# Expert weights fetched by GpSimd's indirect DMAs in place of the sync engine's queue, with GpSimd's loop written out

## The chip, the core and the metric

The kernel runs on one core of a Trainium2 chip. The metric is device time in microseconds (us), from the first to the last instruction of one execution. Five engines take part, each with its own instruction stream: TensorE (PE, the matmuls), VectorE (DVE), ScalarE (ACT), GpSimd (POOL) and the sync engine (SP, which here only issues DMAs). They wait for each other through semaphores.

## What is computed

Six blocks work on 2048 token vectors of 128 numbers: a mixture of experts, causal attention, the mixture again, a block with windowed attention and 32 experts, an encoder block, and the window block once more. The change touches the 32 experts of the window block, which therefore run twice. Cut to what matters, with `h2` the normed tokens:

```python
glogits = h2 @ gate_w + gate_b
topv, topi = jax.lax.top_k(glogits, TOPK)              # 4 of 32 experts for each token
gw = jax.nn.softmax(topv, axis=-1)
combine = zeros((N, 32)).at[arange(N)[:, None], topi].add(gw)
def body(acc, we):                                     # one expert: W_up[e], W_down[e], combine[:, e]
    wu, wd, ce = we
    ug = h2 @ wu                                       # 128 -> 256
    u, g = ug[:, :128], ug[:, 128:]
    return acc + ce[:, None] * (silu(g) * u @ wd), None
y2, _ = jax.lax.scan(body, zeros_like(h2), (W_up, W_down, combine.T))
```

Every expert is applied to every token, and `combine` (mostly zeros) weighs the result.

## The kernel before

Tokens lie along the free axis, in four chunks of 512 (`NCH`, `NC`). A **step** of `experts` (line 541) is one expert on one chunk, so an expert has four steps, and 32 experts have 128. Steps are numbered here from the start of an even expert: steps 0 to 3 are its own, 4 to 7 those of the next expert. Each step keeps fp32 precision by splitting every operand into a high and a low part and adding three products.

- **PE**, line 660, `up`: six matmuls into `gate_up` (two buffers); line 675, `down`: three matmuls that add to `y`. In the loop `up(j+3)` stands ahead of `down(j)`. `up` waits for the product of two steps before (line 656) and, at an expert's first step, for `w_low` (line 654); `down` waits for the low part of `hidden` (lines 669 to 673).
- **ACT**, in each step: `silu(j+1)` (line 696), then the high part of `hidden` of step j, `high(j)` (line 714). At an expert's first step it also makes `w_high` of the next expert (line 703), after a wait for that expert's weights; at its third step `down_high` (line 708).
- **DVE**, in each step: the product of the two halves (line 737); in odd steps the low part of the step before, `low(j-1)` (line 598); then the multiplication by the expert's share, `hidden(j)` (line 744).
- **POOL**: in odd steps `low(j)` (line 598), after a wait for `high(j)`; at an expert's first step `w_low` of the next expert (line 375), at its third `down_low` (line 380). It runs a loop over pairs of experts, with the last pair written out.
- **SP**: for each expert the two parts of its weights (`ExpertParts.load`, lines 346 and 349, 128 KB and 64 KB) and the 1 MB broadcast of its share (line 617). Each is sent when its slot of two is free: the weights when the low parts of the expert two before have been made, the share when `hidden` of that expert is done.

The router (line 388), which runs just ahead, loads and cuts expert 0 through `load_first`, `high_of_first` and `low_of_first`. `mixture` uses the same functions for 8 larger experts and a shared one; there the change leaves all as it is.

Of the kernel before, what the change touches and what calls it, by code (L numbers as in the profile page):

```python
# [14 lines left out]
U32 = mybir.dt.uint32  # L15
# [18 lines left out]
class Phase:  # L34
# [4 lines left out]
    def __init__(self, nc, tag):  # L39
        self.nc, self.tag = nc, tag  # L40
# [283 lines left out]
class ExpertParts:  # L324

    def __init__(self, phase, weights, halves):
        self.weights, self.pieces = weights, halves
        self.width, self.down_width = halves * 256, halves * 128  # L330
# [8 lines left out]
        self.down_loaded = [phase.sem(f"down_loaded{s}") for s in range(2)]  # L339
        self.w_high_done, self.w_low_done = phase.sem("w_high_done"), phase.sem("w_low_done")  # L340
        self.down_high_done, self.down_low_done = phase.sem("down_high_done"), phase.sem("down_low_done")

    def load(self, sp, k, slot):
# [5 lines left out]
        sp.dma_start(self.w_down[slot][:], self.weights[bass.ds(k, 1), :, self.width:].rearrange(  # L349
            "e p c -> (e p) c")).then_inc(self.down_loaded[slot], 16)  # L350

    def load_first(self, sp):
        sp.dma_start(self.w[0][:], self.weights[0, :, 0:self.width]).then_inc(self.w_loaded[0], 16)
        sp.dma_start(self.w_down[0][:], self.weights[0, :, self.width:]).then_inc(self.down_loaded[0], 16)

# [185 lines left out]
def experts(nc, tag, sbuf, parts, x, combine_dram, halves, routed, shared, inner=None):  # L541
# [9 lines left out]
    steps = NCH * halves  # L551
# [3 lines left out]
    CUT_AT, CUT_DOWN_AT = 0, 2 * halves  # L555
    with Phase(nc, tag) as p:
# [31 lines left out]

        def last(it, j):

            return isinstance(it, int) and j == left - 1

        def cut_hidden(engine, it, j):

# [17 lines left out]
        @block.sync  # L612
        def _(sp):
            def load_share(k, slot):

                sp.wait_ge(hidden_done, (k - 1) * steps + EXPERT_CREDIT)
                sp.dma_start(share[slot][:], combine_dram[bass.ds(k, 1), :].to_broadcast(
                    [128, T])).then_inc(share_loaded[slot], 16)

            sp.dma_start(share[0][:], combine_dram[0:1, :].to_broadcast([128, T])  # L620
                         ).then_inc(share_loaded[0], 16)
            with sp.Fori(0, pairs - 1) as it:
                for after in (1, 2):
                    parts.load(sp, it * 2 + after, after % 2)
                    load_share(it * 2 + after, after % 2)
            for k in range(routed - 1, total):
                parts.load(sp, k, k % 2)
                load_share(k, k % 2)

        @block.gpsimd  # L630
        def _(pool):
# [61 lines left out]
        def _(act):  # L693
            def silu(it, j):
                act.wait_ge(gate_up_done, it * (2 * steps) + j + 1)
                act.activation(gated[j % SLOTS][:], gate_up[j % 2][:, 0, :], ACT.Silu  # L696
                               ).then_inc(silu_done, 1)

            def cut_weights(loaded, k, slot):

                act.wait_ge(w_loaded[slot], loaded * 16)

                act.activation(w_high[slot][:], w[slot][:], ACT.Copy).then_inc(w_high_done, 1)

            def cut_down(loaded, k, slot):
                act.wait_ge(down_loaded[slot], loaded * 16)
# [433 lines left out]
            dve.wait_ge(added, NCH)  # L1140


def window_block(nc, tag, sbuf, dram, x, h):

    with Phase(nc, tag) as p:
        u = p.sb("u", [128, T])
# [868 lines left out]
def build(nc, dram, out):  # L2015
    Phase.cleared = []
    with ExitStack() as stack:
        sbuf = {}
        for name, shape, dt in [
            ("x", [128, T], F32), ("ident", [128, 128], F32), ("mean_w", [128, 128], F32),  # L2020
            ("zero_bf", [128, NC], BF16), ("iota", [128, 32], F32),
            ("moe_gate", [128, 8], F32), ("moe_bias", [128, 8], F32),
            ("win_norm", [128, 2], F32), ("win_gate", [128, 32], F32), ("win_gate_b", [128, 32], F32),
        ]:
            sbuf[name] = stack.enter_context(nc.sbuf_tensor(name, shape, dt))
        x = sbuf["x"]
# [5 lines left out]
        window_block(nc, "g1", sbuf, dram, x, h)  # L2032
        encoder_block(nc, "b1", sbuf, dram, x, h)
        window_block(nc, "g2", sbuf, dram, x, h)
        with Phase(nc, "store") as p:
            stored = p.sem("stored")
            block = p.block()
# [7 lines left out]
def host_arrays(i):  # L2045

    a = {}
# [97 lines left out]
```

## Time and profile before

| | |
|---|---|
| time, median of 2 runs | 2673.74 us (2672.32 to 2675.15) |
| the profiled execution, span from its first to its last instruction | 2676.0 us |
| PE busy | 2414.5 us (90%) |
| DVE busy | 2018.5 us (75%) |
| ACT busy | 1425.3 us (53%) |
| POOL busy | 831.3 us (31%) |
| the two runs of the 32 experts | about 1150 to 1420 us and 2400 to 2670 us of the span |
| steady state in them, PE's three `down` matmuls of one step to those of the next | 2.04 us, so 8.16 us an expert |

In the page an idle time is followed by what ended it. Busy shares are means over the whole span; what an edit in the experts is worth is read from a stretch inside them. The profile gives no time of its own beside the span; the span is 2.3 us above the median of the runs.

### The profile page before, as it was taken

How to read it: one execution, taken by the hardware profiler on the slowest of the kernel's cores; microseconds unless marked ns; L12 is line 12 of the kernel's file. 1: busy time of each engine (PE TensorE's matmuls, PEld its weight loads, DVE VectorE, ACT ScalarE, POOL GpSimd, SP SyncE). 2: the span in 40 equal slices, each digit the busy share in tenths (PEclk: the TensorE clock that was granted, in tenths of full speed). 3: DMA queues.
4: the chain of work that ended last, by engine and by line, in shares of the span. 5: the costliest groups of instructions: out<-in, count | busy, mean ns of one | idle time of the engine just before them, and what ended most of it. 6: DMA issues, size and time to landing. Idle time of an engine off the chain costs nothing. (4 is left out here: it accounts for less than half of the span.)

```text
span 2676.0 us, 39008 instructions
## 1 busy us (share of the span) xinstructions
PE 2414.5 (90%) x12429; PEld 1458.6 (55%) x12429; DVE 2018.5 (75%) x4042; ACT 1425.3 (53%) x3042; POOL 831.3 (31%) x813
## 2 busy tenths in 40 slices
PE   9995999869988999899996599999669899989998
PEld 6872333248865555478884422222146555458887
DVE  5985777449988999278886188888349899639888
ACT  4652456626623877156664047667511578526665
POOL 3644222216544000146665100000006200016665
PEclk9997899989999999899998789999889999989999
DMA  2213111022130000034442601010222000014443
GB/s 90 86 38 100 30 42 42 7 86 87 59 87 5 1 1 1 11 135 157 156 148 53 168 17 40 22 40 5 35 44 64 5 1 1 9 44 150 149 149 125
DMA packets 104852, 166.68 MB, mean 62 GB/s; under 512 B 55170, under 2 KB 77570, under 8 KB 92850
## 3 DMA queue, kind: packets, MB, share of 16 engines
q1 hardware_dynamic: 87812, 162.77, 19.4%
q10 hardware_dynamic: 16896, 2.10, 0.5%
q8 instruction: 77, 1.26, 0.2%
q14 instruction: 67, 0.55, 0.1%
HBM read 145.36 MB, written 12.78 MB: 59 GB/s over the span
## 5 line engine op out<-in xcount | busy, mean ns | idle before, releaser
L1623 DVE TENSOR_REDUCE b1x_maxima<-b1x_m_bank 128x1 f32<-128x512 f32 x512 | 319.3, 683 | 59.6 <-PE b1x_m_bank L1557 58.7
L1643 ACT ACTIVATE b1x_probs<-b1x_e_bank 128x1024 f32<-128x1024 f32 x256 | 248.3, 1021 | 143.9 <-PE b1x_e_bank L1574 143.8
L1623 DVE TENSOR_REDUCE a1x_maxima<-a1x_m_bank 128x1 f32<-128x512 f32 (+3 forms) x384 | 191.3, 549 | 59.6 <-PE a1x_m_bank L1560 30.7
L1643 ACT ACTIVATE a1x_probs<-a1x_e_bank 128x1024 f32<-128x1024 f32 (+1 forms) x192 | 146.2, 812 | 132.1 <-PE a1x_e_bank L1574 131.9
L1557 PE MATMUL b1x_m_bank<-b1a_k_slot,b1a_q_slot 96*128 96x512 bf16 x512 | 186.7, 404 | 12.1 <-DMA b1a_q_slot<-scratch_q_parts 11.9
L1574 PE MATMUL b1x_e_bank<-b1a_q_slot,b1a_k_slot 128*128 128x512 bf16 x512 | 153.8, 383 | 1.5 <-DMA b1a_q_slot<-b1x_max_parts 0.5
L1557 PE MATMUL a1x_m_bank<-a1a_k_slot,a1a_q_slot 96*128 96x512 bf16 (+3 forms) x384 | 120.6, 351 | 21.3 <-POOL a1x_mask L1508 12.1
L1589 PE MATMUL b1x_o_bank<-b1x_probs,b1a_v_aug 128*32 128x512 f32 x1024 | 136.4, 605 | 0.4 <-ACT b1x_probs L1643 0.4
L598 POOL TENSOR_TENSOR g1e_low<-g1e_hidden,g1e_high 128x512 fp32r<-128x512 f32 x63 | 109.3, 1735 | 82.0 <-ACT g1e_high L714 82.0
L598 POOL TENSOR_TENSOR g2e_low<-g2e_hidden,g2e_high 128x512 fp32r<-128x512 f32 x63 | 109.3, 1735 | 82.0 <-ACT g2e_high L714 82.0
L1557 PEld LDWEIGHTS b1x_m_bank<-b1a_k_slot,b1a_q_slot 96*128 96x128 bf16 x512 | 41.6, 97 | 167.8 <-DVE b1x_maxima L1623 128.9
L744 DVE TENSOR_TENSOR g1e_hidden<-g1e_hidden,g1e_share 128x512 f32<-128x512 f32 x128 | 114.0, 890 | 3.5 <-DMA g1e_share<-scratch_combine 1.2
L744 DVE TENSOR_TENSOR g2e_hidden<-g2e_hidden,g2e_share 128x512 f32<-128x512 f32 x128 | 114.0, 890 | 3.5 <-DMA g2e_share<-scratch_combine 1.1
L696 ACT ACTIVATE g2e_gated<-g2e_gate_up 128x512 f32<-128x512 f32 x128 | 76.6, 598 | 70.7 <-PE g2e_gate_up L660 70.7
L696 ACT ACTIVATE g1e_gated<-g1e_gate_up 128x512 f32<-128x512 f32 x128 | 76.6, 598 | 70.7 <-PE g1e_gate_up L660 70.7
L1515 POOL CAST b1x_max_parts<-b1x_rest 16x128 bf16<-16x128 f32 x16 | 4.5, 281 | 352.4 <-DVE b1x_rest L1619 352.4
L737 DVE TENSOR_TENSOR g2e_hidden<-g2e_gate_up,g2e_gated 128x512 f32<-128x512 f32 x128 | 87.6, 685 | 25.5 <-ACT g2e_gated L696 25.3
L737 DVE TENSOR_TENSOR g1e_hidden<-g1e_gate_up,g1e_gated 128x512 f32<-128x512 f32 x128 | 87.6, 685 | 25.4 <-ACT g1e_gated L696 25.3
L660 PE MATMUL g1e_gate_up<-g_h_high,g_w_high 128*128 128x512 f32 x256 | 100.2, 391 | 1.0 <-DVE g1e_hidden L737 1.0
L660 PE MATMUL g2e_gate_up<-g_h_high,g_w_high 128*128 128x512 f32 x256 | 100.1, 391 | 1.0 <-DVE g2e_hidden L737 1.0
L1528 POOL TENSOR_SCALAR_AFFINE_SELECT a1x_probs<-a1x_probs 128x256 f32<-128x256 f32 x128 | 51.4, 407 | 156.9 <-ACT a1x_probs L1643 156.2
L660 PE MATMUL g2e_gate_up<-g_h_low,g_w_high 128*128 128x512 f32 x256 | 99.6, 389 | 0.0
(598 smaller groups left out, 6750.7 us busy)
## 6 DMA issues: line engine op xcount, KB each, us to landing
g1e_share<-scratch_combine SPq DMA_DIRECT2D x32, 1024.0 KB, 4.9
g2e_share<-scratch_combine SPq DMA_DIRECT2D x32, 1024.0 KB, 4.9
f1e_share<-scratch_combine SPq DMA_DIRECT2D x9, 1024.0 KB, 4.8
f2e_share<-scratch_combine SPq DMA_DIRECT2D x9, 1024.0 KB, 4.8
g_w<-in_win_experts SPq DMA_DIRECT2D x64, 128.0 KB, 4.4
b1e_window<-scratch_bias_table SPq DMA_DIRECT2D x16, 320.0 KB, 4.6
f_w<-in_moe_w SPq DMA_DIRECT2D x18, 256.0 KB, 4.8
a1a_k_slot<-scratch_k_parts SPq DMA_DIRECT2D x24, 192.0 KB
```

The costliest lines, as they stand in the source:

```text
L598: engine.tensor_tensor(low[s][:], hidden[s][:], high[s][:], ALU.subtract).then_inc(low_done[j % BY_POOL == BY_POOL - 1 and not last(it, j) ...
L660: mm = pe.matmul(gate_up[j % 2][:, which, :], a[slot][:, at], b[:, chunk(n)], start=(part == 0), stop=(part == 2))
L696: act.activation(gated[j % SLOTS][:], gate_up[j % 2][:, 0, :], ACT.Silu).then_inc(silu_done, 1)
L737: dve.tensor_tensor(hidden[s][:], gate_up[j % 2][:, 1, :], gated[s][:], ALU.mult).then_inc(product_done, 1)
L744: dve.tensor_tensor(hidden[s][:], hidden[s][:], share[slot][:, chunk(n)], ALU.mult).then_inc(hidden_done, 1)
L1515: pool.tensor_copy(into[:, 0, :], rest[:]).then_inc(cut, 1)
L1528: pool.affine_select(square, square, [[0, 2], [1, 128]], ALU.is_ge, 0.0, base=0, channel_multiplier=-1).then_inc(cleared, 1)
L1557: mm = pe.matmul(bank[:, 0:width], q_slot[s][0:MAX_ROW, qt // 4, hh, chunk(qt % 4, 128)], k_slot[s][0:MAX_ROW, hh, k0:k0 + width], start=T ...
L1574: mm = pe.matmul(e_bank[pair][:, a, 0:width], k_slot[s][:, hh, chunk(kt, 128)], q_slot[s][:, qh, hh, lo - qh * NC:], start=True, stop=True)
L1589: mm = pe.matmul(o_bank[32 * hh:32 * hh + 32, at:at + width], v_aug[:, half // 2, kt, chunk(hh, 32)], probs[u % 2][:, hh, 0:width], start= ...
L1623: dve.tensor_reduce(maxima[:, k0 // NC, col:col + 1], bank[:, 0:width], AX, ALU.max).then_inc(m_taken, 1)
L1643: act.activation(probs[u % 2][:, 2 * pair:2 * pair + 2, 0:width], e_bank[pair][:, :, 0:width], ACT.Exp, scale=scale).then_inc(exp_done, 1)
```

## The change

`ExpertParts` gets two tables in device memory for the window block's experts: `win_up`, 32 x 128 rows of 256 numbers, and `win_down`, 32 x 128 rows of 128. A new SBUF tensor, `expert_rows`, loaded at the program's start, holds for expert k in column k the 128 row numbers. `gather`, run by GpSimd, fetches the weights of expert k by two indirect DMAs, each of which takes a row number for each of the 128 partitions. Expert 0 is still loaded by SP. SP keeps the shares. GpSimd's program for these experts is written out over all 128 steps in place of the loop; the gathers of expert k+2 stand in expert k's third step, behind `down_low`. Two pairs of semaphores that are never cleared count the gathers, so the second window block adds the counts of the first.

```diff
+    def gather(self, pool, rows, k, slot):
+        pool.wait_ge(self.w_low_done, self.pieces * (k + 1))
+        pool.indirect_dma_start(out=self.w[slot][:], out_offset=None, in_=self.tables[0][:, :],
+                                in_offset=bass.IndirectOffsetOnAxis(ap=rows[:, k:k + 1], axis=0)
+                                ).then_inc(self.w_gathered[slot], 16)
+        pool.wait_ge(self.down_low_done, k + 1)
+        pool.indirect_dma_start(out=self.w_down[slot][:], out_offset=None, in_=self.tables[1][:, :],
+                                in_offset=bass.IndirectOffsetOnAxis(ap=rows[:, k:k + 1], axis=0)
+                                ).then_inc(self.down_gathered[slot], 16)
...
             with sp.Fori(0, pairs - 1) as it:
                 for after in (1, 2):
-                    parts.load(sp, it * 2 + after, after % 2)
+                    if parts.tables is None:
+                        parts.load(sp, it * 2 + after, after % 2)
                     load_share(it * 2 + after, after % 2)
...
-            pair_steps(pool, step)
+            if parts.tables is None:
+                pair_steps(pool, step)
+                return
+            parts.gather(pool, sbuf["expert_rows"], 1, 1)
+            for k in range(total):
+                for j in range(k % 2 * steps, k % 2 * steps + steps):
+                    step(k // 2, j, k + 1 if k + 1 < total else None)
+                    if j % steps == CUT_DOWN_AT and k + 2 < total:
+                        parts.gather(pool, sbuf["expert_rows"], k + 2, k % 2)
...
             def cut_weights(loaded, k, slot):
-                act.wait_ge(w_loaded[slot], loaded * 16)
+                if parts.tables is None:
+                    act.wait_ge(w_loaded[slot], loaded * 16)
+                else:
+                    act.wait_ge(parts.w_gathered[slot], loaded_after_first(loaded, slot) * 16 + parts.gathered_before[slot])
                 act.activation(w_high[slot][:], w[slot][:], ACT.Copy).then_inc(w_high_done, 1)
...
-        parts = ExpertParts(p, dram["win_experts"], halves=1)
+        parts = ExpertParts(p, None, halves=1, tables=(dram["win_up"], dram["win_down"]),
+                            gathered=gathered)
...
-    a["win_experts"] = f(np.concatenate([up[:, :, 128:], up[:, :, :128], g("W_down")], axis=2))
+    a["win_up"] = f(np.concatenate([up[:, :, 128:], up[:, :, :128]], axis=2).reshape(32 * 128, 256))
+    a["win_down"] = f(g("W_down").reshape(32 * 128, 128))
+    a["expert_rows"] = (np.arange(128)[:, None] + 128 * np.arange(32)[None, :]).astype(np.uint32)
```

On POOL, inside the first window block's experts, the loop body of one pair of experts stood so before (`g_w_low` and `g_down_low` are the next expert's low parts, `g1e_low` is `low(j)` of an odd step):

```order
L375 TENSOR_TENSOR g_w_low<-g_w,g_w_high 128x256
L597 ISA
L598 TENSOR_TENSOR g1e_low<-g1e_hidden,g1e_high 128x512
L380 TENSOR_TENSOR g_down_low<-g_w_down,g_down_high 128x128
L597 REGISTER_ALU
L598 TENSOR_TENSOR g1e_low<-g1e_hidden,g1e_high 128x512
L374 REGISTER_ALU
```

These rows are the first of the two experts. With the change the block begins with the gathers of expert 1, and then the first expert's steps stand so:

```order
L358 DMA g_w<-in_win_up,expert_rows 128x256
L362 DMA g_w_down<-in_win_down,expert_rows 128x128
L393 TENSOR_TENSOR g_w_low<-g_w,g_w_high 128x256
L616 TENSOR_TENSOR g1e_low<-g1e_hidden,g1e_high 128x512
L398 TENSOR_TENSOR g_down_low<-g_w_down,g_down_high 128x128
L358 DMA g_w<-in_win_up,expert_rows 128x256
L362 DMA g_w_down<-in_win_down,expert_rows 128x128
L616 TENSOR_TENSOR g1e_low<-g1e_hidden,g1e_high 128x512
```

Two DMAs have come between `down_low` and the `low` of each expert's last step; the register instructions and the branch of the loop are gone.

On SP, in the same block, half of the loop body was this before:

```order
L346 ISA
L346 DMA g_w<-in_win_experts 128x256
L349 ISA
L349 DMA g_w_down<-in_win_experts 128x128
L616 ISA
L617 ISA
L617 DMA g1e_share<-scratch_combine 128x2048
```

With the change the whole body for two experts is this:

```order
L640 ISA
L635 ISA
L635 DMA g1e_share<-scratch_combine 128x2048
L634 ISA
L635 ISA
L635 DMA g1e_share<-scratch_combine 128x2048
L640 REGISTER_ALU
L640 COMPARE_AND_BRANCH
```

Only the shares are left on SP's queue.

## Rows read from the trace of the kernel before

**Rows 1.** The page's first lines: span, then busy time, share and instructions by engine.

```profile
span 2676.0 us, 39008 instructions
...
PE 2414.5 (90%) x12429; PEld 1458.6 (55%) x12429; DVE 2018.5 (75%) x4042; ACT 1425.3 (53%) x3042; POOL 831.3 (31%) x813
```

**Rows 2.** Stretches inside the experts: length, busy time by engine, PE's granted clock, DMA.

```profile
core 0: us, PE busy (x) PEld busy (x) DVE busy (x) ACT busy (x) POOL busy (x), PEclk, DMA share, GB/s
1225.00:1290.00 65.00, 65.00 (x289) 53.81 (x288) 57.97 (x80) 41.39 (x81) 42.61 (x33) 1.00 0.44 153
...
2410.00:2660.00 250.00, 249.78 (x1102) 206.43 (x1101) 223.04 (x307) 159.63 (x307) 165.05 (x123) 1.00 0.42 149
```

**Rows 3.** Who waited for whom, 1160 to 1410 us: total, times, longest.

```profile
POOL g1e_low L598 <- ACT g1e_high L714: 80.1, 62, 1.3
...
PE g1e_y L675 <- POOL g1e_low L598: 0.2, 1, 0.2
```

**Rows 4.** Timeline of PE, two matmuls: start, length, line, tiles.

```profile
1230.54 0.39 PE L675 MATMUL g1e_y<-g1e_high,g_down_high 128*128 128x512 f32 x1
...
1238.70 0.39 PE L675 MATMUL g1e_y<-g1e_high,g_down_high 128*128 128x512 f32 x1
```

**Rows 5.** Timeline of POOL over one expert: start, length, idle before and releaser.

```profile
1226.05 0.90 POOL L380 TENSOR_TENSOR g_down_low<-g_w_down,g_down_high 128x128 fp32r<-128x128 f32 x1
1228.24 1.74 POOL L598 TENSOR_TENSOR g1e_low<-g1e_hidden,g1e_high 128x512 fp32r<-128x512 f32 x1 [1.29 <-ACT g1e_high L714]
1230.20 1.02 POOL L375 TENSOR_TENSOR g_w_low<-g_w,g_w_high 128x256 fp32r<-128x256 f32 x1 [0.21 <-ACT g_w_high L703]
1232.51 1.74 POOL L598 TENSOR_TENSOR g1e_low<-g1e_hidden,g1e_high 128x512 fp32r<-128x512 f32 x1 [1.29 <-ACT g1e_high L714]
1234.21 0.90 POOL L380 TENSOR_TENSOR g_down_low<-g_w_down,g_down_high 128x128 fp32r<-128x128 f32 x1
```

**Rows 6.** Timeline of DVE over the same expert.

```profile
1226.56 0.94 DVE L744 TENSOR_TENSOR g1e_hidden<-g1e_hidden,g1e_share 128x512 f32<-128x512 f32 x1
1227.42 0.68 DVE L737 TENSOR_TENSOR g1e_hidden<-g1e_gate_up,g1e_gated 128x512 f32<-128x512 f32 x1
1228.14 0.69 DVE L744 TENSOR_TENSOR g1e_hidden<-g1e_hidden,g1e_share 128x512 f32<-128x512 f32 x1
...
1229.94 0.68 DVE L598 TENSOR_TENSOR g1e_low<-g1e_hidden,g1e_high 128x512 fp32r<-128x512 f32 x1
1230.54 1.23 DVE L744 TENSOR_TENSOR g1e_hidden<-g1e_hidden,g1e_share 128x512 f32<-128x512 f32 x1
1231.69 0.68 DVE L737 TENSOR_TENSOR g1e_hidden<-g1e_gate_up,g1e_gated 128x512 f32<-128x512 f32 x1
1232.40 0.69 DVE L744 TENSOR_TENSOR g1e_hidden<-g1e_hidden,g1e_share 128x512 f32<-128x512 f32 x1
```

**Rows 7.** POOL's subtractions: count, shortest, median and longest in ns.

```profile
L598 POOL TENSOR_TENSOR g1e_low<-g1e_hidden,g1e_high x63: 1289/1740/1821, 1159.2 to 1411.5; 128x512 fp32r<-128x512 f32 x63
...
L380 POOL TENSOR_TENSOR g_down_low<-g_w_down,g_down_high x64: 457/903/930, 1134.2 to 2656.1; 128x128 fp32r<-128x128 f32 x64
```

**Rows 8.** SP's issues of the weights (ns), and these weights' landing.

```profile
L346 SPq DMA_DIRECT2D g_w<-in_win_experts x62: 332/333/738, 1150.8 to 2642.0; - x62
...
DMA to landing us min/median/max: 2.1/4.4/6.9
```

**Rows 9.** Timeline of SP's queue over the same expert.

```profile
1227.67 0.33 SPq L617 DMA_DIRECT2D g1e_share<-scratch_combine  x1
1228.54 0.33 SPq L346 DMA_DIRECT2D g_w<-in_win_experts  x1
```

**Rows 10.** Timeline of ACT over the same expert.

```profile
1229.71 0.41 ACT L703 ACTIVATE g_w_high<-g_w 128x256 fp32r<-128x256 f32 x1
1230.74 0.60 ACT L696 ACTIVATE g1e_gated<-g1e_gate_up 128x512 f32<-128x512 f32 x1 [0.61 <-PE g1e_gate_up L660]
1231.80 0.63 ACT L714 ACTIVATE g1e_high<-g1e_hidden 128x512 fp32r<-128x512 f32 x1 [0.46 <-DVE g1e_hidden L744]
```

**Rows 11.** Timeline of the first window block's start, ACT and POOL.

```profile
1156.49 0.40 ACT L703 ACTIVATE g_w_high<-g_w 128x256 fp32r<-128x256 f32 x1
...
1156.97 0.94 POOL L375 TENSOR_TENSOR g_w_low<-g_w,g_w_high 128x256 fp32r<-128x256 f32 x1 [22.29 <-ACT g_w_high L703]
```

**Rows 12.** Timeline of the program's start: the last two loads of constants.

```profile
3.67 0.43 SPq L108 DMA_DIRECT2D win_gate<-in_win_gate  x1
...
4.15 0.43 SPq L108 DMA_DIRECT2D win_gate_b<-in_win_gate_b  x1
```

More of the change, by code:

```diff
@@ L324, with __init__ @@
 class ExpertParts:
-    def __init__(self, phase, weights, halves):
+    def __init__(self, phase, weights, halves, tables=None, gathered=None):
         self.weights, self.pieces = weights, halves
+        self.tables = tables
         self.width, self.down_width = halves * 256, halves * 128
@@ L339, in __init__ @@
         self.down_loaded = [phase.sem(f"down_loaded{s}") for s in range(2)]
+        if tables is not None:
+            self.w_gathered, self.down_gathered, self.gathered_before = gathered
         self.w_high_done, self.w_low_done = phase.sem("w_high_done"), phase.sem("w_low_done")
@@ L350, in load @@
             "e p c -> (e p) c")).then_inc(self.down_loaded[slot], 16)
+    def gather(self, pool, rows, k, slot):
[7 more added lines that the diff above has]
+                                ).then_inc(self.down_gathered[slot], 16)
     def load_first(self, sp):
+        if self.tables is not None:
+            sp.dma_start(self.w[0][:], self.tables[0][0:128, :]).then_inc(self.w_loaded[0], 16)
+            sp.dma_start(self.w_down[0][:], self.tables[1][0:128, :]).then_inc(self.down_loaded[0], 16)
+            return
         sp.dma_start(self.w[0][:], self.weights[0, :, 0:self.width]).then_inc(self.w_loaded[0], 16)
@@ L589, in last @@
         def last(it, j):
-            return isinstance(it, int) and j == left - 1
+            return isinstance(it, int) and it == (total - 1) // 2 and j == left - 1
         def cut_hidden(engine, it, j):
@@ L623, in _ @@
                 for after in (1, 2):
-                    parts.load(sp, it * 2 + after, after % 2)
+                    if parts.tables is None:
+                        parts.load(sp, it * 2 + after, after % 2)
                     load_share(it * 2 + after, after % 2)
             for k in range(routed - 1, total):
-                parts.load(sp, k, k % 2)
+                if parts.tables is None:
+                    parts.load(sp, k, k % 2)
                 load_share(k, k % 2)
@@ L639, in step @@
                     cut_hidden(pool, it, j)
-            pair_steps(pool, step)
+            if parts.tables is None:
+                pair_steps(pool, step)
+                return
+            parts.gather(pool, sbuf["expert_rows"], 1, 1)
[4 more added lines that the diff above has]
+                        parts.gather(pool, sbuf["expert_rows"], k + 2, k % 2)
         @block.tensor
@@ L697, in silu, with loaded_after_first @@
                                ).then_inc(silu_done, 1)
+            def loaded_after_first(loaded, slot):
+                return loaded - 1 if slot == 0 else loaded
             def cut_weights(loaded, k, slot):
-                act.wait_ge(w_loaded[slot], loaded * 16)
+                if parts.tables is None:
+                    act.wait_ge(w_loaded[slot], loaded * 16)
+                else:
+                    act.wait_ge(parts.w_gathered[slot], loaded_after_first(loaded, slot) * 16 + parts.gathered_before[slot])
                 act.activation(w_high[slot][:], w[slot][:], ACT.Copy).then_inc(w_high_done, 1)
             def cut_down(loaded, k, slot):
-                act.wait_ge(down_loaded[slot], loaded * 16)
+                if parts.tables is None:
+                    act.wait_ge(down_loaded[slot], loaded * 16)
+                else:
+                    act.wait_ge(parts.down_gathered[slot], loaded_after_first(loaded, slot) * 16 + parts.gathered_before[slot])
                 act.wait_ge(down_done, k * steps - steps + EXPERT_CREDIT)
@@ L1140, in _, with window_block @@
             dve.wait_ge(added, NCH)
-def window_block(nc, tag, sbuf, dram, x, h):
+def window_block(nc, tag, sbuf, dram, x, h, gathered):
     with Phase(nc, tag) as p:
@@ L2023, in build @@
             ("win_norm", [128, 2], F32), ("win_gate", [128, 32], F32), ("win_gate_b", [128, 32], F32),
+            ("expert_rows", [128, 32], U32),
         ]:
@@ L2031, in build @@
         mixture(nc, "f2", sbuf, dram, x, h)
-        window_block(nc, "g1", sbuf, dram, x, h)
+        w_gathered = [nc.alloc_semaphore(f"w_gathered{s}") for s in range(2)]
+        down_gathered = [nc.alloc_semaphore(f"down_gathered{s}") for s in range(2)]
+        window_block(nc, "g1", sbuf, dram, x, h, (w_gathered, down_gathered, (0, 0)))
         encoder_block(nc, "b1", sbuf, dram, x, h)
-        window_block(nc, "g2", sbuf, dram, x, h)
+        window_block(nc, "g2", sbuf, dram, x, h, (w_gathered, down_gathered, (15 * 16, 16 * 16)))
         with Phase(nc, "store") as p:
```

## The prediction

> **What bounds the kernel now.** I read the busy shares first: PE 90% of the span, POOL 31% [rows 1]. A mean over six blocks does not say what the 32 experts wait for, so the next view is that of stretches inside them. There PE is busy for 65.00 of 65.00 us, and for 249.78 of 250 us in the second window block, at a granted clock of 1.00, which is the 2.4 GHz level; POOL works 42.61 of 65 us [rows 2]. The table of waits says the same from the other side: in 250 us PE waited once, for 0.2 us, on POOL's `low`, while POOL waited 62 times for ACT's `high`, 80.1 us in all, 1.3 us each [rows 3]. So the experts are bound by PE, and the loads that the change takes from SP cost PE nothing today. A gain can hardly come out of them. What the change can do is use up POOL's waiting, and the question is how much of it there is at the place where the gathers stand.
>
> The timelines of one expert answer that. PE starts `down(3)` at 1230.54 and `down(7)` at 1238.70, so an expert takes 8.16 us [rows 4]. POOL ends `down_low` at 1226.05 + 0.90 = 1226.95, waits 1.29 us for ACT's `high(3)`, and starts `low(3)` at 1228.24 [rows 5]. That `low(3)` takes 1.74 us, though the shortest of its kind takes 1.289 us [rows 7]. The DVE row beside it says why: `hidden(4)` starts at 1228.14 and ends at 1228.83 [rows 6], and 1228.83 + 1.15 = 1229.98 is where `low(3)` ends. The same shows the other way: DVE's `hidden(5)` takes 1.23 us where `hidden(4)` takes 0.69, and it ends 0.55 us behind the end of POOL's `w_low` at 1231.22 [rows 5, 6]. POOL's subtractions and those DVE operations whose inputs both lie in SBUF hold each other up for whole instructions; the DVE product of line 737, which reads PSUM, is not held up. The Trainium skill has this as a rule ("SBUF — State Buffer", the section on engine contention: a DVE instruction with two SBUF inputs contends with a GpSimd instruction that reads SBUF, and the later one waits); the trace agrees.
>
> **The chain through POOL.** From one `down_low` to the next the work is tied together: `low(3)`, then DVE's `low(4)`, which waits for it, `w_low`, `hidden(5)`, which waits for that, product(6), `hidden(6)` (1232.40, 0.69), `low(5)`, which gets on only at 1233.09 and ends at 1234.25, DVE's `low(6)`, and the next `down_low`, which ends at 1235.11 [rows 5, 6]. From 1226.95 that is 8.16 us. The only slack on POOL's side of this ring is between 1226.95 and 1228.83, when `low(3)` really gets going: 1.88 us. Two gathers that together take G us are hidden up to G = 1.88; each microsecond beyond moves `low(3)`, and with it the rest of the ring, by one. PE's own margin does not help twice: `low(3)` ends at 1229.98 and `down(3)` starts at 1230.54 [rows 4, 5], 0.56 us that are used up once, at the first expert or two, while the ring loses time at each expert.
>
> **The change, part by part.**
>
> *The gathers' time on POOL.* No row of this trace has a DMA issued by POOL, so g, the time of one gather, is bounded. From below: SP issues the same load in 0.333 us [rows 8]. From above: the longest instruction that POOL repeats here, 1.74 us [rows 5]. For what lies between I go by POOL's own rows: undisturbed, 128 columns take 0.457 us and 512 take 1.289 us [rows 7]. I count a gathered row as four such columns (read the row number, work out the address, write the source, write the destination); 128 rows are then 512 columns, and g = 1.3 us. It is a choice, and the largest unknown here. I take the same for both gathers, since both have 128 rows: G = 2.6 us, with ends of 0.67 and 3.48 us. The excess is 2.6 - 1.88 = 0.72 us an expert. Gathers stand in 30 experts of each window block, so 60 x 0.72 = 43 us. A page alone has a price: the Trainium skill ("DMA: Bandwidth & Descriptors", table at the head) gives about 1 us to the first byte for a DMA issued by GpSimd against 0.6 us for one by SP; by that figure taken as g, G would be 2.0 and the sum 60 x 0.12 = 7 us, 2681 us in all.
>
> *The place in the order.* Behind the gathers on POOL stand `low(3)`, for which PE's `down(3)` waits, and `w_low`. Each gather also waits for a low part that POOL itself made an expert earlier, so those waits are met.
>
> *When the weights land.* SP sends the next weights at 1228.54, over 9 us before ACT's `w_high` of that expert could use them [rows 9, 10]: the load at 1228.54 is for the slot that is read one expert later. With the change the weights of expert k+2 are asked for at 1226.95, and ACT wants them at 1229.71. ACT can wait: it idles 0.61 us before `silu(6)`, and DVE takes that result only at 1231.69, 0.35 us after it is ready [rows 6, 10]. So `w_high` may start at 1230.75 at no cost. The gather's descriptors are out at 1226.95 + 1.3 = 1228.25. From there the transfer takes between 2.1 - 0.33 = 1.8 us (alone) and 4.4 - 0.33 = 4.1 us (the median, behind a 1 MB share) [rows 8]. The share is sent at 1227.67 [rows 9] on another queue, so the two overlap instead of standing in line; I take 2.2 us, nearer to the undisturbed row. It lands at 1230.45: free. `w_down` is wanted two steps later.
>
> *The start of each block.* POOL is idle for 22 us before its first `w_low`, and ACT needs expert 1's weights at 1156.49 [rows 11], so expert 1's gathers are hidden by that wait; without it they would cost G once a block.
>
> *SP and the loop.* Two issues fewer an expert on SP free nobody: SP's share still goes out when `hidden` is done. The register instructions and branches that POOL drops lay in its 1.29 us of waiting; no row charges them.
>
> *The constants.* One load more at the start, where issues follow each other by 0.48 us [rows 12] and all are waited for: +0.5 us.
>
> **The sum**: 43 + 0.5 = 43.5 us on a span of 2676.0, so 2719.5. The span stands 2.3 us above the median of the runs, so the time is forecast at 2717 us, +1.6%. About 2% is what a measurement of this kernel can tell from no change; 2% is 53.5 us, or 0.89 us an expert, G = 2.77.
>
> **The rivals.**
>
> 1. *The gathers are hidden.* G up to 1.9, g up to 0.95: 2674 us, with the 0.5 us of constants. For it: 1.88 us without work at that very place [rows 5, 6], and an SP issue of a third of a microsecond. Against it: POOL's shortest instruction in the loop takes 0.457 us for 128 columns, and two gathers must fit.
> 2. *Slower: POOL's ring becomes the bound by more than 2%.* One mechanism, g above 1.39 us. At the upper end, G = 3.48, the excess is 1.60 us and 60 x 1.60 = 96 us, 2770 us. Something is given back there: gathers that end behind 1229.94 let DVE's `low(4)` (0.68 us [rows 6]) go ahead of `low(3)` instead of behind it, so that the excess may be G - 2.5, 0.98 us, 59 us and 2733 us. For it: g = 1.3 is only 0.09 us below the point where it decides.
> 3. *The weights come late.* They land behind the share, 4.1 us after the descriptors, at 1232.35. ACT then holds `silu(6)` and `high(5)` up by 1232.35 - 1230.75 = 1.6 us an expert; that runs beside the 0.7 us on POOL and is not added to it: 96 us, 2770 us. For it: the median landing [rows 8]. Against it: a queue of its own.
> 4. *The gathers are held up as the subtractions are.* If writing the descriptors needs what DVE's two-input operations hold, the gathers wait for `hidden(3)` until 1227.50 and for `hidden(4)`, 0.69 us [rows 6]: 0.55 + 0.69 = 1.24 us more, 60 x 1.96 = 118 us, 2792 us. The Trainium skill warns of just this ("SBUF — State Buffer", "DVE blocks DMA"): descriptors that GpSimd writes starve while DVE runs in a two-port mode; the same page says that `tensor_tensor` has no such mode, and DVE runs only that here. No run here shows it yet.
>
> **How the numbers follow.** Chances: hidden 0.25; forecast (G from 1.9 to 2.77, 2675 to 2727 us) 0.30; ring beyond 2% 0.28; late weights 0.07; starved gathers 0.08; a gain that no row shows 0.02. Within 2% is 0.25 + 0.30 = 0.55, slower 0.28 + 0.07 + 0.08 = 0.43, faster 0.02. The range goes from 2672 us (hidden, with the spread of the runs) to 2795 us (starved gathers); gathers far above 1.74 us each are left outside. The forecast's own range is 2675 to 2727 us.
>
> **What would show it.** POOL's rows for the gathers: 1.3 us each, two an expert; its wait for ACT before `low(3)` gone; PE's `down(3)` now waiting for POOL's `low` about 60 times; the time from `down(3)` to `down(7)` grown from 8.16 to about 8.9 us. A wait of ACT's `w_high` for a DMA would speak for rival 3, gathers of very uneven length beside DVE's `hidden` for rival 4, an unchanged 8.16 us for rival 1. The forecast falls if g is far from 1.3 us, or if DVE and POOL fall into another order so that the ring no longer carries a delay on whole.

## The result: 6% slower, and where the time is

The changed kernel takes 2835.96 us (median of 2 runs, 2832.78 to 2839.14) against 2673.74 us before: a ratio of 1.061, 95% interval 1.0576 to 1.0643, or +162 us. That is outside the range that was given (2672 to 2795 us). The likeliest case was not the one that came; rival 3, the late weights, was, and it cost more than the price it had been given.

The page's head, stretches in both window blocks, and the table of waits in the first of them, to be read beside [rows 1 to 3]:

```profile
span 2837.4 us, 38387 instructions
...
PE 2476.3 (87%) x12364; PEld 1440.8 (51%) x12429; DVE 2119.6 (75%) x4042; ACT 1410.8 (50%) x3042; POOL 892.6 (31%) x937
```

```profile
core 0: us, PE busy (x) PEld busy (x) DVE busy (x) ACT busy (x) POOL busy (x), PEclk, DMA share, GB/s
...
1180.00:1420.00 240.00, 205.70 (x801) 143.49 (x802) 199.29 (x222) 110.09 (x222) 139.23 (x134) 1.00 0.31 116
2520.00:2770.00 250.00, 213.49 (x831) 148.86 (x832) 207.79 (x232) 114.51 (x230) 145.37 (x139) 1.00 0.31 116
```

```profile
ACT g_w_high L738 <- DMA g_w<-in_win_up,expert_rows: 73.6, 23, 3.5
...
PE g1e_y L703 <- POOL g1e_low L616: 27.0, 23, 1.2
PE g1e_gate_up L688 <- DVE g1e_hidden L775: 7.7, 16, 0.7
```

PE was busy for all but 0.2 us of such stretches before [rows 2]; now it works 205.70 of 240 us, at the same granted clock of 1.00. PE itself waits for POOL's `low` and DVE's product, as if POOL were to blame. The longest wait of the table stands one step up: ACT waits for the gathered weights once an expert, 73.6 us in 23 waits. Over both blocks it is 196.9 us in 62. The rows of the gathers (shortest, median and longest in ns) and of the landing, which is counted from the start of the issue, say how:

```profile
L358 POOL DMA_INDIRECT g_w<-in_win_up,expert_rows x62: 1232/1239/1885, 1154.4 to 2809.0; - x62
...
  DMA g_w<-in_win_up,expert_rows: 196.9, 62
...
DMA to landing us min/median/max: 2.2/5.7/7.4
```

```profile
L362 POOL DMA_INDIRECT g_w_down<-in_win_down,expert_rows x62: 944/1001/1081, 1156.6 to 2810.5; - x62
```

A gather of `w` occupies POOL for 1.24 us, one of `w_down` behind it for 1.00, and the weights land 5.7 us after the first one starts. Before, they landed 4.4 us after SP's issue [rows 8] and could afford it, since SP sent them an expert earlier. One expert on POOL, ACT, DVE and SP:

```profile
1242.11 1.23 POOL L358 DMA_INDIRECT g_w<-in_win_up,expert_rows  x1 [0.15 <-issue]
1243.65 1.00 POOL L362 DMA_INDIRECT g_w_down<-in_win_down,expert_rows  x1 [0.30 <-issue]
1244.66 1.28 POOL L616 TENSOR_TENSOR g1e_low<-g1e_hidden,g1e_high 128x512 fp32r<-128x512 f32 x1
1248.29 0.74 POOL L393 TENSOR_TENSOR g_w_low<-g_w,g_w_high 128x256 fp32r<-128x256 f32 x1 [2.35 <-ACT g_w_high L738]
1249.30 1.29 POOL L616 TENSOR_TENSOR g1e_low<-g1e_hidden,g1e_high 128x512 fp32r<-128x512 f32 x1 [0.27 <-ACT g1e_high L752]
1252.08 0.77 POOL L398 TENSOR_TENSOR g_down_low<-g_w_down,g_down_high 128x128 fp32r<-128x128 f32 x1 [1.49 <-ACT g_down_high L746]
1253.00 1.24 POOL L358 DMA_INDIRECT g_w<-in_win_up,expert_rows  x1 [0.15 <-issue]
```

```profile
1247.80 0.42 ACT L738 ACTIVATE g_w_high<-g_w 128x256 fp32r<-128x256 f32 x1 [3.30 <-DMA g_w<-in_win_up,expert_rows]
...
1251.17 0.63 ACT L752 ACTIVATE g1e_high<-g1e_hidden 128x512 fp32r<-128x512 f32 x1 [1.46 <-DVE g1e_hidden L782]
```

```profile
1249.46 1.67 DVE L782 TENSOR_TENSOR g1e_hidden<-g1e_hidden,g1e_share 128x512 f32<-128x512 f32 x1
```

```profile
1242.69 0.33 SPq L635 DMA_DIRECT2D g1e_share<-scratch_combine  x1
```

An expert is now a ring of another kind. The gather starts at 1242.11; its weights reach ACT at 1247.80, 5.69 us later; ACT then makes `w_high` and `silu(6)`, DVE the product and `hidden(6)`, ACT `high(6)` and `down_high`, POOL `down_low`, and at 1253.00, 5.20 us later, the next gather starts: 10.89 us instead of 8.16 (the following one takes 10.48). POOL no longer is what it waits for: it idles 2.35 us for `w_high` alone. And SP issues the share, 1 MB, from 1242.69 to 1243.02, while POOL is still busy with the gather until 1243.35. In what follows, a transfer's descriptors (the list of what the DMA engines are to move) are taken to be out when its issue ends.

What the DMA engines do meanwhile is in the view of the queues, here for two stretches, 1243.35 to 1246.5 us and 1246.5 to 1248 us; q0 is POOL's queue, q1 SP's:

```profile
DMA packets 124, 1.02 MB, mean 322 GB/s; under 512 B 0, under 2 KB 0, under 8 KB 0
...
q1 hardware_dynamic: 124, 1.02, 76.2%
```

```profile
DMA packets 100, 0.23 MB, mean 153 GB/s; under 512 B 48, under 2 KB 48, under 8 KB 96
...
q0 software_dynamic: 80, 0.20, 33.0%
q1 hardware_dynamic: 20, 0.03, 6.1%
```

From 1243.35 us, when POOL is done with the gather of `w`, to 1246.5 us the engines move 124 packets, all of them the share's, which has 128. Then, to 1248 us, come POOL's 80, those of `w` and `w_down` together. The two transfers did not share the time between them; the gather stood behind nearly the whole share. The Trainium skill ("DMA: Bandwidth & Descriptors", the section on SWDGE, HWDGE and iDMA) says that each DMA engine takes the queues of the two kinds in turn. The rows contradict that only if a turn is shorter than an engine's part of the share, 8 of the 128 packets on each of 16 engines; no run here measures how long a turn is.

### The profile page after: what moved, and what is told of

Same layout as the page of the kernel before. It is cut to its first block and busy times, and to the rows that moved or that the text cites. A ratio compares the mean times of both kernels' runs of the same rounds, so it can differ in the third digit from the quotient of the medians.

```text
span 2837.4 us, 38387 instructions
## 1 busy us (share of the span) xinstructions
PE 2476.3 (87%) x12364; PEld 1440.8 (51%) x12429; DVE 2119.6 (75%) x4042; ACT 1410.8 (50%) x3042; POOL 892.6 (31%) x937
## 5 line engine op out<-in xcount | busy, mean ns | idle before, releaser
L1613 PE MATMUL b1x_e_bank<-b1a_q_slot,b1a_k_slot 128*128 128x512 bf16 x474 | 144.6, 382 | 3.2 <-ACT b1x_probs L1682 0.8
L782 DVE TENSOR_TENSOR g2e_hidden<-g2e_hidden,g2e_share 128x512 f32<-128x512 f32 x128 | 126.6, 989 | 4.4 <-DMA g2e_share<-scratch_combine 2.1
L782 DVE TENSOR_TENSOR g1e_hidden<-g1e_hidden,g1e_share 128x512 f32<-128x512 f32 x128 | 126.6, 989 | 3.1 <-DMA g1e_share<-scratch_combine 0.8
L688 PE MATMUL g2e_gate_up<-g_h_high,g_w_high 128*128 128x512 f32 x256 | 111.0, 434 | 14.8 <-DVE g2e_hidden L775 14.5
L738 ACT ACTIVATE g_w_high<-g_w 128x256 fp32r<-128x256 f32 x62 | 25.9, 418 | 196.9 <-DMA g_w<-in_win_up,expert_rows 196.9
L752 ACT ACTIVATE g2e_high<-g2e_hidden 128x512 fp32r<-128x512 f32 x128 | 80.6, 629 | 85.5 <-DVE g2e_hidden L782 85.5
L752 ACT ACTIVATE g1e_high<-g1e_hidden 128x512 fp32r<-128x512 f32 x128 | 80.6, 630 | 84.2 <-DVE g1e_hidden L782 84.2
L688 PE MATMUL g1e_gate_up<-g_h_high,g_w_high 128*128 128x512 f32 x256 | 111.0, 434 | 12.8 <-DVE g1e_hidden L775 12.3
L688 PE MATMUL g1e_gate_up<-g_h_high,g_w_low 128*128 128x512 f32 x256 | 100.7, 393 | 0.0
```

The lines of the kernel that those rows point to most:

```text
L688: mm = pe.matmul(gate_up[j % 2][:, which, :], a[slot][:, at], b[:, chunk(n)], start=(part == 0), stop=(part == 2))
L752: act.activation(high[j % SLOTS][:], hidden[j % SLOTS][:], ACT.Copy).then_inc(high_done, 1)
L782: dve.tensor_tensor(hidden[s][:], hidden[s][:], share[slot][:, chunk(n)], ALU.mult).then_inc(hidden_done, 1)
L1613: mm = pe.matmul(e_bank[pair][:, a, 0:width], k_slot[s][:, hh, chunk(kt, 128)], q_slot[s][:, qh, hh, lo - qh * NC:], start=True, stop=True)
```

## The experiments

Three theories were to be told apart: the weights come **late**, because the share is ahead of them at the DMA engines; **POOL's time**, that is, the ring of the prediction; and gathers that are slow **by themselves** (held up by DVE, or by their form). The kernel before was timed again beside these kernels, at 2672.9 to 2675.7 us; the ratios are to those times.

| kernel | us | ratio to before, 95% interval | landing of w after its issue, median | ACT's waits for w, both blocks |
|---|---|---|---|---|
| changed kernel | 2835.96 | 1.061 (1.0576 to 1.0643) | 5.7 | 196.9 us |
| e1_ahead | 2727.65 | 1.020 (1.0182 to 1.0218) | 5.7 | 2.9 us |
| e6_share_after | 2736.87 | 1.0235 (1.0217 to 1.0253) | 3.0 | 30.9 us |
| e11_share_later | 2734.23 | 1.0229 (1.0209 to 1.025) | 3.0 | 30.0 us |
| e2_small_share | 2705.22 | one run | 3.9 | 71.8 us |
| e3_sp_behind_share | 2833.01 | 1.0596 (1.0577 to 1.0616) | 4.5 | 200.4 us |
| e4_unroll_only | 2673.14 | 0.9998 (0.9986 to 1.001) | as before | as before |
| e9_plain_pool | 2674.39 | one run | 2.4 | 4.6 us |
| e10_plain_down_first | 2751.29 | 1.0287 (1.0269 to 1.0305) | 3.9 | 120.9 us |
| e8_third_gather | 2779.70 | 1.0391 (1.0356 to 1.0425) | 5.7 | 2.9 us |
| e5_split_ahead | 2677.85 | 1.0009 (0.9995 to 1.0022) | 5.6 | 3.2 us |

### Is it lateness? e1_ahead and e3_sp_behind_share

```diff
             parts.gather(pool, sbuf["expert_rows"], 1, 1)
+            parts.gather(pool, sbuf["expert_rows"], 2, 0)
...
-                    if j % steps == CUT_DOWN_AT and k + 2 < total:
-                        parts.gather(pool, sbuf["expert_rows"], k + 2, k % 2)
+                    if j % steps == CUT_DOWN_AT and k + 3 < total:
+                        parts.gather(pool, sbuf["expert_rows"], k + 3, (k + 1) % 2)
```

> The changed kernel with each gather one expert earlier (expert k+3 in place of k+2 at the same place on POOL; expert 2 ahead of the loop). Same number of gathers, same place in POOL's order. If the loss is the late landing of w (ACT waits 196.9 us for it in the changed kernel): ACT's wait for the gathered w vanishes and POOL's ring is left, 2.24 us of gathers and 0.45 us between them against 1.88 us of room: 0.8 us x 60, about 2723 us, from 2674 to 2735. If it is the time that the gathers take on POOL: unchanged, about 2836 us.

The weights still land 5.7 us after their issue, but an expert ahead of their use, and ACT's wait goes from 196.9 to 2.9 us. The time falls by 108 us to 2727.65 us; 2723 had been expected. What is left, 55 us over before, is dealt with below.

The other way round, the kernel before with its SP loads made late:

```diff
                 for after in (1, 2):
+                    if not shared:
+                        load_share(it * 2 + after, after % 2)
                     parts.load(sp, it * 2 + after, after % 2)
-                    load_share(it * 2 + after, after % 2)
+                    if shared:
+                        load_share(it * 2 + after, after % 2)
```

(`shared` is false for the 32 experts; the last expert likewise, cut here)

> The kernel before (weights by SP, GpSimd's loop, no gather), with one edit: for the 32 experts SP sends the share of expert k ahead of that expert's weights instead of behind it, so the weights go out about where the gathers of the changed kernel do and land behind the share. If lateness alone makes the loss, whoever sends the load: w lands near 1228.1 + 4.4 in the timeline of before, against 1230.75 at the latest; the period becomes about 9.8 us and the time about 2772 us (2740 to 2830). If it takes the gathers' work on POOL or their form: 2674 us.

2833.01 us: the whole loss, without one gather and without a DMA on POOL. So lateness behind the share is enough. It costs more than the 2772 us expected, 3 us above the top of that range, and about what the changed kernel costs. SP's queue and ACT's wait:

```profile
1249.16 0.33 SPq L617 DMA_DIRECT2D g1e_share<-scratch_combine  x1
1249.74 0.33 SPq L346 DMA_DIRECT2D g_w<-in_win_experts  x1
```

```profile
1253.95 0.42 ACT L709 ACTIVATE g_w_high<-g_w 128x256 fp32r<-128x256 f32 x1 [2.96 <-DMA g_w<-in_win_experts]
```

### Why do they land late? e6_share_after, e11_share_later, e2_small_share

```diff
             def load_share(k, slot, times=None):
+                if times is not None:
+                    sp.wait_ge(parts.w_gathered[slot], times * 16 + parts.gathered_before[slot])
                 sp.wait_ge(hidden_done, (k - 1) * steps + EXPERT_CREDIT)
```

(cut: the calls for the 32 experts pass how often the slot has been gathered)

> The changed kernel, but SP sends the 1 MB share of expert k only when the gathered w of expert k has landed. The gathers stay where they are. If w is late because its packets share the DMA engines with the share: w lands about 2 us after its descriptors instead of 4.3, ACT's wait mostly goes, about 2723 us (2690 to 2750). If gathers land late by themselves, with or without the share: unchanged, 2836 us or more. If the loss is POOL's time: unchanged, 2836 us.

The landing falls from 5.7 to 3.0 us: 1.8 us after the descriptors, which is the undisturbed end of the bounds in the prediction. So gathers that are slow by themselves are out as the cause of the long wait; 30.9 us of ACT's 196.9 are left. The time, 2736.87 us, lies in the range expected of the share.

This run puts the share behind the gather's end. The next only puts it behind its descriptors:

```diff
-                sp.wait_ge(hidden_done, (k - 1) * steps + EXPERT_CREDIT)
+                later = 0 if parts.tables is None else 1
+                sp.wait_ge(hidden_done, (k - 1) * steps + EXPERT_CREDIT + later)
```

> The changed kernel with one number: SP sends each share when one step more of hidden is done, about 1.3 us later, so behind the descriptors of the gathered w (out 0.66 us after the share went out in the changed kernel). SP waits for no landing. If the order at the DMA engines decides: w lands about 3 us after its gather starts as in e6_share_after, and POOL's ring is left: about 2730 us, from 2715 to 2750. If the queues take turns: the 1 MB share still lies beside the gather, w lands later than 4 us, above 2760 us.

2734.23 us and again 3.0 us to the landing. One number in SP's wait, 1.3 us later for the share, takes back 102 of the 162 us. The same bytes are moved; the order in which the two transfers come to the engines decides how long `w` waits.

```diff
-                sp.dma_start(share[slot][:], combine_dram[bass.ds(k, 1), :].to_broadcast(
-                    [128, T])).then_inc(share_loaded[slot], 16)
+                cols = T if parts.tables is None else 128
+                sp.dma_start(share[slot][:, 0:cols], combine_dram[bass.ds(k, 1), 0:cols].to_broadcast(
+                    [128, cols])).then_inc(share_loaded[slot], 16)
```

(cut: ahead of the loop SP also loads one whole share into the second slot and waits for it)

> The changed kernel with the shares of experts 1 to 31 cut to their first 128 of 2048 columns (64 KB instead of 1 MB; the rest of the shares keeps what an earlier load left, so this leaves a part of the computation's input out). If w is late for sharing the DMA engines with the 1 MB share: w lands about 3.3 us after the gather starts instead of 5.7, about 2723 us (2690 to 2750). If gathers land late by themselves or for DVE's work: unchanged, about 2836 us.

A share of a sixteenth, sent at the old place, gives a landing of 3.9 us and 2705.22 us in one run. The share still goes in 128 packets, of 512 bytes instead of 8 KB, so the number of its packets alone does not make the weights late; its size counts. That this run is faster than e6 and e11, though ACT waits longer in it, was not expected; it comes back below.

### Does the indirect form matter? e9_plain_pool, e10_plain_down_first

```diff
-        pool.indirect_dma_start(out=self.w[slot][:], out_offset=None, in_=self.tables[0][:, :],
-                                in_offset=bass.IndirectOffsetOnAxis(ap=rows[:, k:k + 1], axis=0)
-                                ).then_inc(self.w_gathered[slot], 16)
+        pool.dma_start(self.w[slot][:], self.tables[0][k * 128:k * 128 + 128, :]).then_inc(self.w_gathered[slot], 16)
```

(the same for `w_down`)

> The changed kernel with plain DMAs of the same 128 rows from GpSimd's queue in place of the indirect ones, at the same place. If the place and the share make the loss: 2800 to 2840 us, the same wait of ACT for w. If the indirect form makes it (row numbers, one descriptor a row): below 2730 us.

2674.39 us in one run, and the first case of the expectation fell: with the same place on POOL and the same share there is no loss. The rows say why it fell.

```profile
L358 POOL DMA_DIRECT2D g_w<-in_win_up x62: 559/559/711, 1150.4 to 2644.3; - x62
...
DMA to landing us min/median/max: 2.0/2.4/6.7
```

```profile
1243.33 0.56 POOL L358 DMA_DIRECT2D g_w<-in_win_up  x1
1243.89 0.53 POOL L360 DMA_DIRECT2D g_w_down<-in_win_down  x1
```

```profile
1244.10 0.33 SPq L631 DMA_DIRECT2D g1e_share<-scratch_combine  x1
```

A plain DMA takes POOL 0.56 us instead of 1.24, and here as in e11_share_later POOL's first packet moves 0.71 us after the end of its issue. The descriptors of `w` are out at 1243.89, 0.54 us ahead of the share's, whose issue ends at 1244.43; those of an indirect DMA would have come at 1244.57, 0.14 us behind them. The indirect form matters by its length: it loses a race that the plain one wins. Both plain DMAs together, 1.09 us, also fit into POOL's 1.88 us.

To test this, the plain pair was turned round, so that `w` goes out 0.5 us later, level with the share: in one expert SP's issue of the share runs from 1240.81 to 1241.14, and POOL's of `w` ends at 1241.13.

```diff
+        pool.wait_ge(self.down_low_done, k + 1)
+        pool.dma_start(self.w_down[slot][:], self.tables[1][k * 128:k * 128 + 128, :]).then_inc(self.down_gathered[slot], 16)
         pool.wait_ge(self.w_low_done, self.pieces * (k + 1))
         pool.dma_start(self.w[slot][:], self.tables[0][k * 128:k * 128 + 128, :]).then_inc(self.w_gathered[slot], 16)
-        pool.wait_ge(self.down_low_done, k + 1)
-        pool.dma_start(self.w_down[slot][:], self.tables[1][k * 128:k * 128 + 128, :]).then_inc(self.down_gathered[slot], 16)
```

> e9_plain_pool (plain DMAs from GpSimd's queue) with one edit: w_down is sent ahead of w, so the descriptors of w are out 0.53 us later, 1.1 us after POOL starts, when SP has already sent the share (0.77 us after POOL's start in e9_plain_pool). If the DMA engines finish the transfer that reached them first before they begin the next one: w lands behind the share, ACT waits for it, about 2830 us, from 2760 to 2840. If the two queues take turns, or if the indirect form alone made the loss: 2674 us.

2751.29 us, ACT waits 120.9 us: the loss comes back with plain DMAs, but only half of it, and below the range expected. The landing is 3.9 us, between 2.4 and 5.7. The expectation had counted to the start of SP's issue (0.77 us after POOL's start); counted to its end, 0.33 us later, the edit makes the two level and does not put `w` behind. Up to 1242 us only POOL's packets move, 39 of them; from 1242.5 to 1243 us the view of the queues shows packets of both kinds:

```profile
DMA packets 23, 0.14 MB, mean 279 GB/s; under 512 B 0, under 2 KB 0, under 8 KB 12
...
q1 hardware_dynamic: 11, 0.09, 45.8%
q0 software_dynamic: 12, 0.05, 24.6%
```

With the two so close, part of POOL's packets got ahead. How that fell out engine by engine stays open; so does what it costs `w` that `w_down`, 64 KB, now stands ahead of it in POOL's own queue. From end of issue to end of issue, in one expert of each: the share is 0.33 us ahead in the changed kernel (landing 5.7 us), level here (3.9), 0.54 us behind in e9 (2.4), 1.00 us behind in e11 (3.0, and again indirect).

### What is left: POOL's ring. e8_third_gather, e5_split_ahead, e4_unroll_only

With the weights in time, e1, e6 and e11 lie 55 to 64 us above the kernel before, and PE waits for POOL's `low`, as the prediction had it; from 1180 to 1400 us of e1_ahead:

```profile
PE g1e_y L704 <- POOL g1e_low L616: 11.8, 24, 0.5
```

To measure that ring, e1_ahead was given a third gather:

```diff
                         parts.gather(pool, sbuf["expert_rows"], k + 3, (k + 1) % 2)
+                        pool.indirect_dma_start(out=spare[:], out_offset=None, in_=parts.tables[1][:, :],
+                                                in_offset=bass.IndirectOffsetOnAxis(
+                                                    ap=sbuf["expert_rows"][:, k:k + 1], axis=0)
+                                                ).then_inc(spared, 16)
```

(cut: POOL first waits for the landing of the third gather of the expert before; that wait was always met)

> e1_ahead with a third gather of 128 rows of 512 bytes into a tile that nobody reads, behind the other two, in 58 experts. It measures the ring's slope. If each microsecond of POOL beyond 1.88 us an expert moves the ring by one: 58 x (1.00 + 0.30) = 75 us more than e1_ahead, about 2803 us, from 2785 to 2815. If DVE and POOL fall into an order that gives a part back (low(4) ahead of low(3)): 2760 to 2785 us. If the ring is not what costs e1_ahead its 55 us: 2728 us.

2779.70 us: 52 us more, or 0.90 us an expert for 0.95 + 0.30 us of POOL. The ring carries time on, but not whole; that is the second case of the expectation. The order did change:

```profile
1245.73 0.68 DVE L619 TENSOR_TENSOR g1e_low<-g1e_hidden,g1e_high 128x512 fp32r<-128x512 f32 x1
1246.33 2.80 DVE L793 TENSOR_TENSOR g1e_hidden<-g1e_hidden,g1e_share 128x512 f32<-128x512 f32 x1
```

```profile
1246.61 1.28 POOL L619 TENSOR_TENSOR g1e_low<-g1e_hidden,g1e_high 128x512 fp32r<-128x512 f32 x1
1247.82 0.74 POOL L393 TENSOR_TENSOR g_w_low<-g_w,g_w_high 128x256 fp32r<-128x256 f32 x1
```

DVE's `low(4)` is done before POOL's `low(3)` starts, and `hidden(5)` then waits through two POOL instructions: 2.80 us for what takes 0.69 alone. In e1_ahead it is `low(4)` that waits (1.8 us in most experts, up to 2.46).

Such an order also goes with e2_small_share being the faster one. DVE's `low(4)` in e6_share_after, and then in e2_small_share:

```profile
1249.20 2.45 DVE L616 TENSOR_TENSOR g1e_low<-g1e_hidden,g1e_high 128x512 fp32r<-128x512 f32 x1
```

```profile
1248.17 1.49 DVE L617 TENSOR_TENSOR g1e_low<-g1e_hidden,g1e_high 128x512 fp32r<-128x512 f32 x1
```

In e6 and e11 `w_low` follows `low(3)` on POOL at once, and `low(4)` waits through both, 2.4 to 2.5 us in 60 experts. In e2 the weights come later, POOL idles 0.55 us ahead of `w_low`, and `low(4)` gets in between, 1.5 us in most experts. An expert takes 8.68 us there, against 9.20 in e6 and e11. That the order makes the whole of this difference is not shown.

If the ring is a matter of room at one place, the same two gathers in two places should cost nothing:

```diff
+            parts.gather_up(pool, sbuf["expert_rows"], 2, 0)
...
-                    if j % steps == CUT_DOWN_AT and k + 2 < total:
-                        parts.gather(pool, sbuf["expert_rows"], k + 2, k % 2)
+                    if j % steps == CUT_AT and k + 2 < total:
+                        parts.gather_down(pool, sbuf["expert_rows"], k + 2, k % 2)
+                    if j % steps == CUT_DOWN_AT and k + 3 < total:
+                        parts.gather_up(pool, sbuf["expert_rows"], k + 3, (k + 1) % 2)
```

(against the changed kernel; `gather` cut into its two halves, not shown)

> As e1_ahead, but the two gathers are put in different waits of POOL: w of expert k+3 behind down_low, w_down of expert k+2 behind w_low. Each takes 1.0 to 1.24 us and 0.15 to 0.3 us ahead of it, against 1.88 and about 1.87 us of room. If room on POOL is what is left once the landing is in time: 2674 to 2682 us. If any gather on POOL costs its time: 2740 us or more.

2677.85 us, a ratio of 1.0009 (0.9995 to 1.0022): no loss that can be measured. POOL's timeline, and a stretch (same columns as above):

```profile
1245.35 1.24 POOL L361 DMA_INDIRECT g_w<-in_win_up,expert_rows  x1
1246.61 1.63 POOL L621 TENSOR_TENSOR g1e_low<-g1e_hidden,g1e_high 128x512 fp32r<-128x512 f32 x1
1248.45 1.01 POOL L398 TENSOR_TENSOR g_w_low<-g_w,g_w_high 128x256 fp32r<-128x256 f32 x1 [0.21 <-ACT g_w_high L746]
1249.61 1.24 POOL L367 DMA_INDIRECT g_w_down<-in_win_down,expert_rows  x1
```

```profile
1180.00:1400.00 220.00, 220.00 (x973) 182.15 (x972) 196.25 (x271) 140.34 (x271) 205.48 (x163) 1.00 0.42 153
```

POOL is busy for 205.48 of 220 us, and PE is again busy for all of them. Each gather of 1.24 us fits into a wait that POOL had anyway.

Last, the kernel before with GpSimd's loop written out, and nothing else (cut: the test for the last step, which must now know the expert):

```diff
-            pair_steps(pool, step)
+            if shared:
+                pair_steps(pool, step)
+                return
+            for k in range(total):
+                for j in range(k % 2 * steps, k % 2 * steps + steps):
+                    step(k // 2, j, k + 1 if k + 1 < total else None)
```

> The kernel before with GpSimd's loop written out for the 32 experts and nothing else; SP loads the weights. All theories expect 2674 us, within 5 us: POOL waits 1.29 us for ACT ahead of each low part and no row charges the loop's register instructions. Anything else would make the unrolling part of the loss.

0.9998 (0.9986 to 1.001): it costs and gains nothing that can be measured.

No version beats the kernel before, and [rows 2] say why: PE is busy for the whole of these stretches there.

## Why the prediction was wrong, point by point

- **What bounds the kernel.** Right: nothing was to be gained, and e5 and e9 show that the weights can come from POOL at no cost as long as PE is not kept waiting.
- **The gathers' time on POOL.** Right, in part by luck: 1.3 us each was taken, 2.6 together; 1.24 and 1.00 were measured, with 0.15 and 0.30 us of issue ahead of them, 2.69 in all. The four columns a row were a choice that happened to come out; in e5, where each gather stands alone, `w` and `w_down` take 1.24 us alike.
- **The ring.** Right in kind and nearly in size: 43 us were forecast, 55 us measured where it is alone (e1_ahead). That each microsecond beyond 1.88 costs one came out only roughly: 0.94 us an expert for 0.81 in e1_ahead, 0.90 for the 1.25 of the third gather, with DVE and POOL in other orders; `low(4)` ahead of `low(3)`, as rival 2 had it, is what e8_third_gather shows. It does not add to the late weights: e3, without the gathers, costs as much as the changed kernel. The prediction said so of the two.
- **When the weights land.** This is the step that failed. The prediction had the gather and the share "overlap instead of standing in line" and took 2.2 us from the descriptors to the landing; it was 4.4 us from the end of the issue (1243.35 to 1247.80), more than its upper bound of 4.1 us from [rows 8]. A queue of its own was held to be a reason for overlap. The engines moved the share first, because SP's issue took 0.33 us and began 0.58 us after POOL's, which took 1.24: the share's descriptors were out 0.33 us ahead. With that order turned round (e11_share_later) the landing comes 1.8 us after the end of the issue. The prediction had both times, the share's issue from 1227.67 for 0.33 us [rows 9] and its own 1228.25 for the gather's descriptors, and did not compare them as a race.
- **The price of that rival.** 96 us were given, 162 measured, with a chance of 0.07. Of the 2.7 us an expert, 1.6 are the wait as it was priced. 5.69 us from the gather's start to `w_high`, where 5.40 was priced, add 0.3. From `w_high` to the next gather it takes 5.20 us; the prediction had 4.36 (1230.75 to 1235.11), another 0.8. The row behind that is DVE's `hidden(6)`, 1.67 us instead of 0.69: after ACT's long wait POOL's `low(5)` and DVE's `hidden(6)` become ready almost together, POOL's starts first (1249.30 against 1249.46), and DVE waits for it on the chain. The slacks that the timeline of before showed were those of its own order. e3 was under-priced by the same (2772 for 2833 us): in both kernels 62 of the `hidden` take 1.67 us.
- **Gathers held up by DVE.** Wrong as a rival: the 62 gathers of `w` have a shortest of 1.232 and a median of 1.239 us beside DVE's operations, and only the first of each block is longer, up to 1.885. The Trainium skill's warning of starved descriptors ("SBUF — State Buffer", "DVE blocks DMA") speaks of a mode that it says `tensor_tensor` does not have, and the trace agrees in that these gathers were not held up.
- **The loop, SP's queue, the constants.** Nothing that can be measured (e4_unroll_only 0.9998; e9_plain_pool, which has the extra constant too, 2674.39 us in one run); the 0.5 us forecast for the constants is too small to tell.

## What to carry to other kernels

A load has two numbers, when it is issued and when it is needed; a change of queue that keeps the bytes can take away the distance between them, so compare that distance with the landing time, not with the engine's share. Where two transfers are sent close together, find out whose descriptors are out first: here 128 KB whose descriptors came 0.33 us behind those of 1 MB landed only when the large transfer had ended. And price a new wait with the orders that it makes, not with the slacks of the old timeline.

## What the runs showed of the hardware

- An indirect DMA of 128 rows takes POOL 1.24 us (1 KB and 512 B rows alike, e5_split_ahead), 1.00 us when it follows another and 1.88 to 1.89 us the first time in a block (changed kernel), with 0.15 to 0.30 us of issue ahead; a plain one of the same rows 0.54 to 0.56 us (e9_plain_pool).
- With the share behind them, gathered weights land 3.0 us after the start of the issue, 1.8 us after its end (e6_share_after, e11_share_later); behind a 1 MB share 5.7 us. In the expert shown, 124 of the share's 128 packets went ahead of the first of the gather.
- A DVE operation with two SBUF inputs took 2.80 us instead of 0.69 beside two POOL instructions in a row (e8_third_gather, in 56 experts).
